# Perceiver block on one core: four spread matmuls in one run, and two chunks of the own weights' product placed ahead of the product with hqT

## The reference, cut to what matters

```python
Sim = (encoder_hc @ w1)[:, :, None] + (decoder_hq @ w2)[:, None, :] \
      + jnp.einsum('bid,bjd->bij', encoder_hc * w3, decoder_hq) + b_sim[0]
A = jax.nn.softmax(Sim, axis=2)
hq_hat = jnp.einsum('bij,bjd->bid', A, decoder_hq)
Batt = jax.nn.softmax(jnp.max(Sim, axis=2), axis=1)
hc_bar = jnp.einsum('bi,bid->bd', Batt, encoder_hc)[:, None, :]
hc_hat = jnp.broadcast_to(hc_bar, encoder_hc.shape)
feats = jnp.concatenate([encoder_hc, hq_hat, encoder_hc * hq_hat, encoder_hc * hc_hat], axis=-1)
hcq = feats @ W_qv + b_qv
```

## Time and profile before

| | |
|---|---|
| runs of the kernel | median 1359.72 us of 3 (1355.3 to 1359.99) |
| profiled execution | 1357.04 us, its span 1355.3 us |
| PE busy | 1232.2 us, 91% |
| PE weight loads | 733.4 us, 54% |
| DVE, ACT, POOL busy | 730.2, 337.1, 707.6 us |
| mean granted clock of PE | 0.973 of 2.4 GHz |
| 16 pairs of cross attention | from about 16 to about 686 us of the span |

### The profile page before, as it was taken

One profiled execution on the slowest core, in us unless ns is written; L12 is line 12 of the kernel. 1 busy time (PEld: TensorE's weight loads), 2 busy tenths in 40 slices (PEclk: granted clock), 3 DMA queues, 4 the chain that ended last, 5 costly groups with the idle time before them and its releaser, 6 DMA issues. The chain is left out here.

```text
span 1355.3 us, 29581 instructions
## 1 busy us (share of the span) xinstructions
PE 1232.2 (91%) x10417; PEld 733.4 (54%) x10418; DVE 730.2 (54%) x1573; ACT 337.1 (25%) x768; POOL 707.6 (52%) x762
## 2 busy tenths in 40 slices
PE   0899999999999999999989699999499999999994
PEld 0444434444443444443457456565378888888883
DVE  4555566555566655566259657777733323323325
ACT  2222233232233232233135211111311111111110
POOL 1055544345543445553139656787398553550872
PEclk9999999999999999999979899999599999999997
DMA  8645554434555444555054567863314443321556
GB/s 284 226 146 200 211 209 154 152 145 176 209 209 178 139 153 159 208 210 193 19 191 142 152 204 273 282 208 103 101 51 144 155 155 131 125 100 56 154 161 188
DMA packets 99376, 225.45 MB, mean 166 GB/s; under 512 B 14152, under 2 KB 30664, under 8 KB 95216
## 3 DMA queue, kind: packets, MB, share of 16 engines
q1 hardware_dynamic: 87872, 189.46, 40.9%
q0 software_dynamic: 10288, 33.57, 7.4%
q10 hardware_dynamic: 1152, 1.57, 0.4%
HBM read 179.21 MB, written 45.35 MB: 166 GB/s over the span
## 5 line engine op out<-in xcount | busy, mean ns | idle before, releaser
L326 POOL TENSOR_TENSOR wb<-w,hcb 128x512 f32<-128x512 f32 x120 | 122.1, 1038 | 315.2 <-DVE hcb L683 292.9
L401 PE MATMUL S<-ctxT,x 32*64 32x416 f32 (+1 forms) x4096 | 185.2, 511 | 15.9 <-DVE ctxT L627 15.9
L401 PEld LDWEIGHTS S<-ctxT,x 32*64 32x64 f32 x4096 | 108.5, 133 | 94.8 <-issue 45.8
L329 POOL TENSOR_TENSOR wb<-wb,w 128x512 f32<-128x512 f32 x120 | 150.0, 1271 | 0.0
L609 DVE STREAM_TRANSPOSE ctxT<-ctx_one 128x1024 f32<-128x1024 f32 (+1 forms) x128 | 115.1, 949 | 13.5 <-DMA ctx_one<-in_ctx_dram 13.2
L436 PE MATMUL O<-ctx_one,probsT 128*64 128x512 f32 (+1 forms) x448 | 110.4, 608 | 0.0
L1929 POOL TENSOR_TENSOR w_low<-w_low,w_high 128x2048 fp32r<-128x2048 f32 x21 | 96.7, 4607 | 1.7
L522 ACT ACTIVATE x<-S,w2R,w3R 128x128 f32<-128x128 f32 x256 | 92.7, 472 | 19.5 <-PE S L392 19.5
L2114 DVE TENSOR_TENSOR f_hL<-f_TH,f_hH 128x512 fp32r<-128x512 f32 x39 | 27.0, 692 | 120.4 <-ACT f_hH L2067 117.3
L634 DVE TENSOR_REDUCE mx<-S 128x1 f32<-128x832 f32 x16 | 16.4, 1025 | 128.1 <-PE S L401 128.1
L1452 PE MATMUL Pb<-WrT,yT 128*32 128x128 f32 x2016 | 69.8, 280 | 13.7 <-DVE yT L1705 13.1
(11 more groups left out here) (286 smaller groups left out, 2497.6 us busy)
## 6 DMA issues: line engine op xcount, KB each, us to landing
ctx_one<-in_ctx_dram SPq DMA_DIRECT2D x64, 512.0 KB, 4.5
x<-in_ctx_dram SPq DMA_DIRECT2D x16, 1536.0 KB
ctx_two<-in_ctx_dram SPq DMA_DIRECT2D x16, 1536.0 KB, 9.4
ctx_one<-in_ctx_dram SPq DMA_DIRECT2D x64, 256.0 KB, 5.5
w_low<-_L_ffn_gate_up_proj_dram POOLq DMA_DIRECT2D x10, 1024.0 KB, 8.1
f_xt<-routed_x SPq DMA_DIRECT2D x39, 256.0 KB
routed_y<-f_yt SPq DMA_DIRECT2D x39, 256.0 KB
w_low<-_L_ffn_gate_up_proj_dram SPq DMA_DIRECT2D x6, 1024.0 KB, 8.0
```

What stands on the lines that cost most here:

```text
L326: pool.tensor_tensor(wb[:, slot, b], w3[:, c], hcb[:, c, b, None].to_broadcast([P, D]), ALU.mult).then_inc(wb_step, 1)
L329: pool.tensor_tensor(wb[:, slot, b], wb[:, slot, b], w0[:, c], ALU.add).then_inc(wb_ready, 1)
L401: last = pe.matmul(S[64 * b:64 * b + 64, a, 0:tiles * Q], qr[a * Q:(a + 1) * Q, k, 64 * b:64 * b + 64], ctxT[a * Q:(a + 1) * Q, 0:tiles, b ...
```

## The change

The four spread matmuls of a full step now stand in one run, at n == 2 of `values`; the run of two after the values is gone. The matmul of `brow` stands after position n == 4 in place of n == 5. The chunks 0 and 1 of `own_product` stand ahead of the product with hqT, right behind the four transpositions, and open the sum in Y (`start`). The programs of the other engines are unchanged.

```diff
-            def spread_queries(f, fs, blocks):
+            def spread_queries(f, fs):
...
-                for e in blocks:
+                for e in range(QUADS):
...
-            def product(lhsT, w, chunks, start):
+            def product(lhsT, w, chunks):
...
-                    last = pe.matmul(Y[:], lhsT[:, c, :], w12[:, w + c, :], start=start and c == 0, stop=(w > 0 and c == C - 1))
+                    last = pe.matmul(Y[:], lhsT[:, c, :], w12[:, w + c, :], start=False, stop=(w > 0 and c == C - 1))
...
                         last = pe.matmul(Y[64 * b:64 * b + 64, :], hcT[s][:, c, 64 * b:64 * b + 64], wb[:, c % 2, b, :],
-                                         start=False, stop=False)
+                                         start=c == 0, stop=False)
...
                     if n == 2 and step != "last":
-                        spread_queries(p + 1, 1 - s, (0, 1))
+                        spread_queries(p + 1, 1 - s)
...
-                    if n == 5:
+                    if n == 4:
...
                     values(p, s, step)
-                    if front:
-                        spread_queries(f, fs, (2, 3))
                     pe.wait_ge(hqh_ready, p + 1)
                     turn_tile(0, "hqh", tok_rows, p, step)
...
                     pe.wait_ge(hcb_step, p + 1)
+                    own_product(p, s, range(half))
                     pe.wait_ge(hqT_ready, p + 1)
-                    product(hqT, 0, range(C), True)
-                    own_product(p, s, range(half))
+                    product(hqT, 0, range(C))
```

More of the change, by code:

```diff
@@ L466, in body @@
                     turn_tokens(f)
-                    spread_queries(f, fs, range(QUADS))
+                    spread_queries(f, fs)
                 if front:
@@ L473, in body @@
                     pe.wait_ge(t_free[0], turn(0, "hqh", p, step) + 1)
-                    product(f3, C, range(half), False)
+                    product(f3, C, range(half))
                     own_product(p, s, range(half, C))
@@ L479, in body @@
                 if back:
-                    product(f3, C, range(half, C), False).then_inc(y_done, 1)
+                    product(f3, C, range(half, C)).then_inc(y_done, 1)
                 if front:
```

## The result

| | before | changed |
|---|---|---|
| median of 20 runs each | 1356.53 us (1353.98 to 1361.30) | 1361.48 us (1357.99 to 1369.22) |
| ratio to before | | 1.0039, 95% interval 1.0026 to 1.0053 |
| span of the profiled execution | 1355.3 us | 1363.1 us |
| PE busy | 1232.2 us | 1224.3 us |
| last product of the cross attention ends | 686.2 us | 692.1 us |

What follows compares the result with a forecast made beforehand. One PE chain through the cross attention was taken to bound the kernel: 15 pairs at +0.50 us and -0.8 in the last make +6.7, giving 1363.7 on the profiled execution and 1366.4 on the median; middle 1365, range 1359.5 to 1371.5.

Steps and rivals of the forecast that it cites:

- What bounds: Cross attention: one chain on PE, busy 39.47 of 40.24 us a pair, with POOL a side chain ending late.
- The 1.56 us of air: Before the change, POOL done with chunks 0 and 1 at 316.71, PE taking chunk 0 at 318.27.
- The second spread run: Behind the values: its removal moves the transpositions from 313.24 to 313.04, 0.20 us gained there.
- The run of four: First spread run: four matmuls run beside each other and cost no more than two; 0.01 us taken, upper end 0.96.
- brow a position earlier: In the values: brow's matmul moves from 305.61 to 304.75, 0.86 us, and the DVE, hcb, POOL chain moves whole.
- The wait: PE between chunks 0 and 1: idle 1.44 us for POOL; chunk 1 ready at 315.85, hop 0.15, start 316.00.
- Chunk 1 to the scores: On PE: 1.01 us for chunk 1 and change to the product, then 3.61 for the product and change behind it.
- The period: From one spread run to the next: 0.49 us longer, 0.50 with the wider spread run, against 40.24 before.
- The sum: Cross attention: fifteen full pairs at +0.50 us make +7.5, the last pair -0.8, together +6.7 us.
- the dear run of four: Rival at the spread run: four matmuls cost more than two, up to 0.96 us a pair, 14.4 more; chance 0.05.
- the falling clock: Rival on PE: waits close together lower the clock once a pair, 15 x 1.7 = 26 us; chance 0.04.
- In time: Rival at chunk 1: weights ready when chunk 0 is done, scores 0.95 us earlier, 15 us over 16 pairs; chance 0.07.

Runs made afterwards that it cites:

- Chunk 0 alone in front: Changed kernel with only chunk 0 ahead of the product with hqT, chunk 1 behind it: 1342.25 us, ratio 0.9904 to the kernel before.
- the light chunk 1: Changed kernel with POOL's addition of w0 for chunk 1 cut to one column: periods of 39.25 and 39.33 us; total of 1351.38 us not read.
- DVE's chunk 0: Changed kernel with DVE making chunk 0, used ahead of the transpositions, and POOL starting with chunk 1, used behind them: 1329.39 us, ratio 0.9798 to the kernel before.
- the run alone: Kernel before with only the four spread matmuls put in one run at n == 2: periods of 40.05 and 40.13 us, ratio 0.9987.

## Why the prediction was right

It said 1365.0 (1359.5 to 1371.5), most likely within 0.5% and on the slow side; measured are 1361.48 and +0.39%, with the whole interval above zero. The mechanism it named, a new wait for POOL's second chunk, is the one the trace shows and the experiments move. By its steps:

- *What bounds.* One chain on PE, with POOL's end beside it: right. Chunk 0 alone in front, the light chunk 1 and DVE's chunk 0 take the wait away in three ways, and each time the period falls. The 1.56 us of air were misread: 316.71 is the end of chunk 1, and PE took chunk 1 not at 318.27 but 0.86 later, at 319.13, so the air was 2.42. The sum did not use the 1.56; it set chunk 1's end against chunk 1's place.
- *The second spread run, 0.20.* The transpositions stand 0.79 behind the values' end, and the run alone brought 0.11 to 0.19 a pair. In the changed kernel it brought nothing, since chunk 1 waits for POOL longer than that.
- *The run of four, 0.01.* 1.07 for 1.06. Eight rows last 1.14 us where they lasted 2.09 in the first step, so the reading that the first step ran slow was right, 1.8 times as it did for the transpositions. The 1.00 in the clock column there has no record under it: the first record of the clock in that trace starts at 40.7 us. The prediction's estimate of 0.26 more, from the 3.07 that the Trainium skill gives in "TensorE: Matmul & The Clock Gate", section "Measured speedup vs the span model", did not come true on this shape. It also set four against one matmul, where the change sets four against two.
- *brow a position earlier, 0.86.* Spread run to brow's matmul 3.79, predicted 3.79. DVE's start without a new wait: right, 0.52 behind.
- *The wait.* Spread run to chunk 1: 15.00, predicted 15.04. The hop was sized at 0.15 from the start of POOL's next operation and is 0.11 from there (318.86 to 318.97); POOL's last operation for chunk 1 ends 0.05 behind that start, and from this end to PE it is 0.05 in every pair. The 1.44 us were a gap from chunk 0's streaming end; the row gives 1.25, since a matmul's row lasts longer than its streaming, and from start to start it is 2.33 - 0.86 = 1.47.
- *Chunk 1 to the scores.* 318.97 to 323.61 is 4.64, predicted 4.62. The unseen change of tiling cost 0.02 more than the row that stood for it. The Trainium skill, "TensorEngine Tiling (Array Packing)", section "Key Properties", says that the engine drains at a change of the tiling mode; the trace agrees with that in so far as this change is about as dear as the 0.15 and 0.2 of the others.
- *The period.* 40.71 to 40.73 in twelve pairs, predicted 40.74; 40.52 in the first and 40.53 in the last, where POOL is 0.18 quicker, which the sum did not allow for.
- *The sum.* 6.7 was expected for the cross attention, 5.9 came (686.2 to 692.1; 4.9 in the second trace), and 4.9 between the medians. The 15 full pairs made 6.6 and not 7.5: three with 0.29 and not 0.50, where POOL is quicker (0.6 us), and twelve with 0.48 (0.3 us). The last pair gained 1.0 and not 0.8. And the first full step starts 0.3 later than in the trace of before, but 0.8 earlier in the second trace of the changed kernel. That is scatter of the start, where the change moves nothing, and it brought this trace closer to 6.7 by luck. The medians stand lower than the three runs that I had: 1356.5 for 1359.7, so the middle that I took was 2 us too high. Two of the prediction's prices were also added up wrong, and neither entered the range: the dear run of four stands at 1378 and 1381, not 1377 and 1380, and the falling clock at 1389, since the 26 us come on top of the waits' 6.7.
- *The rivals.* "In time" needed chunk 1 0.49 us sooner; it wasn't, and with it sooner (the light chunk) the gain came as worked out, 0.91 to 0.99 for 0.95. The falling clock did not show in two traces of this kernel, but at about 0.7 us more of waiting it did, in single pairs, at 1.69 us a time for the 1.7 it was priced at; its chance of 0.04 was low for how near it was.

## What to carry to other kernels

Before work is moved into a wait, look up when each of its own inputs is ready, not only the first: here chunk 0 was ready and chunk 1 was not, and moving one chunk in place of two turns +0.4% into -1.0%. A gap that another engine's end leaves today (2.42 us of air for chunk 1 here) is a budget: the product of 3.6 us that stood in front of the chunks was what kept it. And where the side chain ends late, its own work can be shared out: giving a quarter of it to an engine with room, and putting what that engine makes into PE's other wait, took the gain from 1.0% to 2.0%.

## What the runs showed of the hardware that I had not expected

- PE's clock is nearer to its edge than an average of 1.00 tells. With waits of 0.79 and 1.25 us in a pair it stayed at 2.4 GHz; with one of 1.92 it fell to 1.2 GHz in five of 15 pairs, with 0.79 and 2.4 in eight of 15, each fall costing 1.7 us. With most of that last wait filled by unused matmuls (0.4 to 0.6 us left) it fell in none. The kernel with more work was 12 us faster, one execution each.
- DVE's operation for a chunk (two inputs and the output in SBUF) takes 0.75 us in the last pair, where POOL is idle, and 1.52 (median of 30) beside POOL's operations of the same kind. POOL's first four took 2.49 and 2.96 in pairs, where such pairs take 2.04 and 2.50 without that DVE operation beside them. The Trainium skill, "SBUF — State Buffer", section "Who interferes with whom", says that a DVE operation with two SBUF inputs and a GpSimd operation that reads SBUF contend for a shared pair of ports, and that the pair is an exclusive lock. The rows agree with that in kind: both are longer. Which of them held the ports when, they don't show. The rows of the run with chunk 0 on DVE:

```profile
297.40 2.49 POOL L327 TENSOR_TENSOR wb<-w,hcb 128x512 f32<-128x512 f32 x2 [20.17 <-DVE hcb L685]
297.50 2.94 DVE L694 SCALAR_TENSOR_TENSOR wb<-w,hcb 128x512 f32<-128x512 f32 x2 [0.26 <-DVE hcb L685]
...
299.85 2.96 POOL L330 TENSOR_TENSOR wb<-wb,w 128x512 f32<-128x512 f32 x2
```
